# Cross attention weights turned on VectorE in 32x32 blocks, value product in sixteen 32x32 tiles of TensorE

## The reference

```
q, k, v = x@Wq.T + bq, x@Wk.T + bk, x@Wv.T + bv
attn    = sigmoid(layernorm(q) @ layernorm(k).T / 16 - log(1024))
x       = layernorm(x + (attn @ v @ Wo.T + bo) * layerscale)

qh, kh, vh = heads(x@wq.T + b), heads(ctx@wk.T + b), heads(ctx@wv.T + b)   # 16 heads of 16
attn    = softmax(qh @ kh.T / 4)                                            # 77 keys
x       = layernorm(x + (attn @ vh) @ dense.T + b)

r   = sigmoid((mu_r*x + (1-mu_r)*x_prev) @ W_r.T)
kk  = relu((mu_k*x + (1-mu_k)*x_prev) @ W_k.T) ** 2
out = layernorm(x + r * (kk @ W_v.T))
```

## Time and profile before

| | |
|---|---|
| median of 3 runs | 535.03 us (534.8 to 535.73) |
| span of the profiled execution | 531.8 us |
| PE busy | 515.0 us (97%), 4530 matmuls |
| ACT busy | 450.4 us (85%) |
| DVE busy | 443.7 us (83%) |
| POOL busy | 381.9 us (72%) |

### The profile page before, as it was taken

One profiled execution on the slowest core, in us unless ns is written; L12 is line 12 of the kernel. 1 busy time (PEld: TensorE's weight loads), 2 busy tenths in 40 slices (PEclk: granted clock), 3 DMA queues, 4 the chain that ended last, 5 costly groups with the idle time before them and its releaser, 6 DMA issues.

```text
span 531.8 us, 12709 instructions
## 1 busy us (share of the span) xinstructions
PE 515.0 (97%) x4530; PEld 468.3 (88%) x4530; DVE 443.7 (83%) x995; ACT 450.4 (85%) x1130; POOL 381.9 (72%) x554
## 2 busy tenths in 40 slices
PE   9999999999999999999999999999999898999994
PEld 6888999898989898989898989999898787899994
DVE  4787868878888879797979797778878888999996
ACT  3765579998989898989898989899999899898965
POOL 1774747676867676767667675767778889897996
PEclk9999999999999999999999999999999999999998
DMA  6410120110010110101010100020511000011122
GB/s 193 128 49 21 38 60 6 42 39 2 14 50 27 35 38 24 42 19 52 12 39 3 39 2 22 21 74 28 166 35 41 2 2 1 22 41 41 41 80 100
DMA packets 23269, 22.50 MB, mean 42 GB/s; under 512 B 1724, under 2 KB 23204, under 8 KB 23205
## 3 DMA queue, kind: packets, MB, share of 16 engines
q1 hardware_dynamic: 22770, 21.35, 12.7%
q10 hardware_dynamic: 434, 0.34, 0.2%
HBM read 14.55 MB, written 6.82 MB: 40 GB/s over the span
## 4 chain that ended last, share of the span: by engine, by line
PE 70%; ACT 12%; DVE 9%; issue 4%; POOL 4%; POOLq 0%; DVEq 0%; ACTq 0%
PE st L298 16%; PE acc L298 14%; PE xb L298 10%; PE proj L298 10%; PE xb L2077 5%; PE xb L2096 5%; ACT p_sb L594 4%; PE xb L2064 4%; DVE xm L1485 3%; ACT L545 2%; PE proj L1973 2%; PE xb L1885 1%; POOL rs L1110 1%; PE st L1893 1%; DVE kkT_lo L1299 1%
## 5 line engine op out<-in xcount | busy, mean ns | idle before, releaser
L594 ACT ACTIVATE p_sb<-xb,neg_mx 128x77 f32<-128x77 f32 x512 | 120.0, 366 | 5.2 <-DVE neg_mx L1412 4.9
L1047 POOL TENSOR_TENSOR fold<-p_sb 128x640 f32<-128x640 f32 x32 | 50.2, 1568 | 75.4 <-ACT p_sb L594 75.1
L1052 POOL TENSOR_TENSOR p_sb<-p_sb,rc 128x1280 f32<-128x1280 f32 x32 | 75.3, 2353 | 23.8 <-DVE rc L1425 23.7
L298 PE MATMUL acc<-vv_hi,aT_hi 128*128 128x256 f32 x256 | 76.6, 299 | 0.0
L545 ACT ACT_TABLE_LOAD x58 | 74.4, 1283 | 1.0
L298 PE MATMUL st<-qkT_hi 128*128 128x256 f32 x256 | 74.8, 292 | 0.0
L298 PE MATMUL st<-qkT_lo,qkT_hi 128*128 128x256 f32 x256 | 72.4, 283 | 0.0
L298 PE MATMUL st<-qkT_hi,qkT_lo 128*128 128x256 f32 x256 | 72.4, 283 | 0.0
L298 PE MATMUL acc<-vv_lo,aT_hi 128*128 128x256 f32 x256 | 72.2, 282 | 0.0
L298 PE MATMUL acc<-vv_hi,aT_lo 128*128 128x256 f32 x256 | 72.2, 282 | 0.0
L1412 DVE TENSOR_REDUCE neg_mx<-xb 128x4 f32<-128x308 f32 x128 | 53.7, 467 | 17.1 <-PE xb L2064 16.7
(11 more groups left out here) (262 smaller groups left out, 1707.9 us busy)
## 6 DMA issues: line engine op xcount, KB each, us to landing
xs<-in_x SPq DMA_DIRECT2D x16, 256.0 KB, 3.0
xraw<-in_xT SPq DMA_DIRECT2D x15, 256.0 KB, 2.9
out_y<-y SPq DMA_DIRECT2D x15, 256.0 KB, 2.1
x_kept<-xs SPq DMA_DIRECT2D x10, 256.0 KB, 2.2
x2s_a<-x_kept SPq DMA_DIRECT2D x2, 512.0 KB, 5.0
x2s_b<-x_kept SPq DMA_DIRECT2D x2, 512.0 KB, 7.1
x2s_c<-x_kept SPq DMA_DIRECT2D x1, 512.0 KB, 3.7
cT<-in_cT SPq DMA_DIRECT2D x1, 308.0 KB, 3.3
```

Of the source, the lines that this page charges most:

```text
L298: mm = pe.matmul(out, s_, m_, start=first and k == 0 and q == 0, stop=last and k == n - 1 and q == 2, skip_group_check=not check)
L594: ex = act.activation(weights(t)[:, h // KH * (H // 2) + KH * n + h % KH, 0:SC], logits[n][:, h * SC:(h + 1) * SC], ACT.Exp, bias=neg_mx[: ...
L1047: pool.tensor_tensor(fold[:].rearrange("p (h k) -> p h k", k=FO), p[:, :, 0:FO], p[:, :, FO:2 * FO], ALU.add).then_inc(fo_pool.sem, 1)
L1052: pool.tensor_tensor(weights(t), weights(t), rc[:, t % 2].rearrange("p (h o) -> p h o", o=1) .to_broadcast([P, H, SP]), ALU.mult).then_inc ...
```

## The change

1. `weights_t`, `weights_body` and both `weights_tail` go. In their place `weights_turn` (DVE, L1548) turns all 128 x 1280 weights of a tile in one instruction, each 32x32 block by itself, from `p_sb` into `pT`. The blocks stay in their group of 32 partitions, so a partition group of `pT` holds the keys for its own 32 tokens only.
2. `mixed` (PE, L2308) therefore works in 32x32 tiles: for each of 2 halves, 5 groups of 32 key slots, 4 groups of tokens and 4 groups of heads there is a matmul of 32 rows into 32 partitions with 64 columns: 160 for a pair where 16 were. The four groups of tokens go to the top 128 columns of the four `xb` banks, beside the logits (308 columns). `vb` grows from 2048 to 5120 elements per partition and holds the values four times, once for each partition group; 24 DMAs fill it.
3. `mixed_hi` and `mixed_lo` read the four banks through a pattern that puts the tokens back in order.
4. `cross_scores` no longer waits for turned weights; `exponentials(t)` waits for `weights_turn(t-2)`; `mixed` waits for all exponentials of the next tile, where it waited for three of four groups.
5. `table_for` issues the table load itself. The number of table loads in the program is 58 (59 before).
6. Every engine's list of calls is written in a new order. The rounds hold the same calls, apart from those above.

```diff
-                        w.wait_ge(*consts_pool.at(0))
-                        n = 8 * (next(spares) % NSPARE)
-                        act.activation(spare[:, n:n + 1], nlogs[:], func)
+                        act.preload_act_table(func)
...
-                        w.wait_ge(*tp_pe.at(t - NP))
+                        w.wait_ge(*tp_dve.at(t - NP))
...
-                def weights_body(t, c):
-                    w.wait_ge(*tp_pe.at(t, c + 1))
+                def weights_turn(t):
+                    w.wait_ge(*pn_pool.at(t))
                     w.wait_ge(*pads_pool.at(0))
...
-                    dve.tensor_copy(pT[:, 4 * c:4 * c + 4, (t % 2) * P:(t % 2 + 1) * P], tiles(tp_bank(c), 4))\
-                        .then_inc(tp_dve.sem, 1)
+                    dve.transpose(pT[:, t % 2], p_sb[:, t % NP]).then_inc(tp_dve.sem, 1)
...
-                    copy(oT[0][:], mixed_bank(i)).then_inc(pv_act.sem, 1)
+                    copy(by_token(oT[0][:]), by_quadrant(mixes_ps)).then_inc(pv_act.sem, 1)
...
                 def mixed(i):
                     b = i // JB
-                    for c in range(3):
-                        w.wait_ge(*turned(2 * i + 1, c))
+                    w.wait_ge(*tp_dve.at(2 * i + 1))
                     w.wait_ge(*vb_dma.at(VB_DMA - 1))
-                    if i < NJ - 2:
-                        w.wait_ge(*ex_act.at(2 * i + 2, 3))
...
+                    w.wait_ge(*ex_act.at(2 * i + 2 if i < NJ - 2 else NT - 1))
+                    if i:
+                        w.wait_ge(*pv_dve.at(i - 1))
+                        w.wait_ge(*xda_dve.at(min(i - 1, NJ - 3)))
                     for k in range(KC):
-                        for half in range(2):
-                            for n in range(4):
-                                mm = pe.matmul(mixed_bank(i)[32 * n:32 * (n + 1), k * D:(k + 1) * D], vb[:, n, half, :, :, KC * b + k].rearrange("p a d -> p (a d)"),
-                                               pT[:, 5 * k + n + half], start=half == 0, stop=half == 1, skip_group_check=True)
+                        for c in range(NC):
+                            for a in range(P // Q):
+                                own = slice(Q * a, Q * (a + 1))
+                                for n in range(NG):
+                                    slots = (NC * (NG * k + n) + c) * Q
+                                    mm = pe.matmul(xb[Q * n:Q * (n + 1), a, MX + 2 * Q * k:MX + 2 * Q * (k + 1)],
+                                                   vb[own, n, c, :, :, KC * b + k].rearrange("p a d -> p (a d)"),
+                                                   pT[own, :, slots:slots + Q], start=c == 0, stop=c == NC - 1, skip_group_check=True)
                     mm.then_inc(pv_pe.sem, 1)
...
                 def round_(r):
-                    at(attend, 4 * r - 18, NS, 9)
-                    at(scores, 4 * r - 15, NS, 13)
...
+                    qk(2 * r + 1)
+                    scores(4 * r - 11)
```

More of the change, by code:

```diff
@@ L89, in value_pieces @@
 def value_pieces():
-    for n in range(4):
[L92 to L98, removed]
+    for a in range(KH):
+        key = 0
+        while key < SC:
+            c, row = divmod(SP * a + key, Q)
+            count = min(Q - row, SC - key)
+            yield a, c, row, key, count
+            key += count
 def decoder_layer(nc, io):
@@ new lines, in _ @@
+                sigmoid_hi(16)
+                v_hi(7)
+                exponentials(4, 0)
+                exponentials(4, 1)
+                for r in range(6, 12):
+                    round_(r)
+                exponentials(16, 2)
+                tqk_hi(27)
+                exponentials(16, 3)
+                sigmoid(41)
+                xt_hi(15)
+                norm2(5)
+                sigmoid(42)
+                mixed_hi(7)
+                sigmoid_hi(41)
+                sigmoid_hi(42)
@@ L1735, in _ @@
-                weights_body(26, 0)
-                sigmoid_lo(61)
-                weights_body(26, 1)
+                qk_bias(16)
+                attended(3)
+                qk_stats(16)
+                sums(4)
+                mixed_lo(1)
+                stats1(3)
+                reciprocals(4)
+                maxima(5, 0)
+                maxima(5, 1)
+                maxima(5, 2)
+                for r in range(5, 11):
+                    round_(r)
+                v_bias(14)
+                qk_norm(28)
@@ new lines, in _ @@
+                qk_norm(31)
+                attended(11)
+                stats1(11)
+                sigmoid_lo(48)
+                sums(20)
+                mixed_lo(9)
+                reciprocals(20)
+                sigmoid_lo(49)
+                maxima(21, 0)
+                maxima(21, 1)
+                tqk_lo(31)
+                maxima(21, 2)
+                maxima(21, 3)
+                stats2(8)
+                sigmoid_lo(50)
+                x1_lo(11)
+                crossed(9)
@@ L2116, in x2 @@
                     if i == ND:
-                        for c in range(3):
-                            w.wait_ge(*turned(NT - 1, c))
+                        w.wait_ge(*pv_dve.at(NJ - 1))
                     elif i:
@@ new lines, in round_ @@
+                    cross_scores(2 * r - 10)
+                    scores(4 * r - 10)
+                    attend(4 * r - 14)
+                    tqk(2 * r + 1)
+                    attend(4 * r - 13)
+                    qk(2 * r + 2)
+                    mixed(r - 6)
+                    v(r + 1)
+                    cross_scores(2 * r - 9)
+                    scores(4 * r - 9)
+                    scores(4 * r - 8)
+                    attend(4 * r - 12)
+                    dense(r - 6)
+                    tqk(2 * r + 2)
@@ L2257, in _ @@
-                cross_scores(0)
                 attend(5)
-                scores(9)
+                attend(6)
+                attend(7)
+                cross_scores(1)
                 tqk(11)
-                attend(6)
                 scores(10)
                 qk(12)
-                cross_scores(1)
-                attend(7)
                 scores(11)
```

1347 lines of the change are left out of this document (750 added, 597 removed).

## The result

The changed kernel took **636.5 us** (median of 4 runs, 633.2 to 639.5) against 535.2 us (534.8 to 535.7): a ratio of **1.189**, interval 1.186 to 1.192. The forecast was 517.6 us in a range of 503 to 547. It is slower by 101 us, more than any rival had it (the worst was 600 us), and the profiled execution has a span of 634.6 us.

What follows compares the result with a forecast made beforehand. PE was taken to bound the kernel (busy 515.0 of 531.8 us). Sixteen pairs gaining 1.09 us each (4.26 less 3.17) save 17.4: span 514.4, plus 3.2 for a run, 517.6 us; range 503 to 547.

Steps and rivals of the forecast that it cites:

- 4.26 us a pair leave PE: On PE, 20 transposes (2.17 us) and the old value product (2.09 us) go from each pair.
- The body of the value product, 2.8 us: PE's 320 records a pair, taken between 2.1 and 3.5 us; with 0.37 for going in and out, 3.2 us.
- Code: PE's instruction fetch: 640 instructions are 2.5 packets at 1.2 us each; three one after the other take 3.5 us.
- the sign, stalls at every 256th instruction: In a value product on PE, starts 7 ns apart with such stalls would show code as the limit.
- Pace: PE issue between different tiles: 7 ns a record, from three gaps in `cross_scores`; 320 records take 2.1 to 2.2 us.
- The forecast's own point of no gain: On PE, a body of 3.9 us, 12 ns a record, from which the change is slower.
- Waits: PE's `mixed` waiting for exponentials fits with little to spare: nothing charged, up to 1 us a round kept in the range.
- rival 4: Gain eaten by `mixed`'s wait, DVE's longer blocks or code fetch: 528 to 533 us, chance 0.11; 535 to 550, chance 0.06.
- The turn: DVE's turn of 1280 elements takes 1.47 us, 47.0 us in all; DVE 22.3 us a middle round.
- SP's 24 DMAs: On SP, filling the larger `vb` takes 17.3 us instead of 8.9, about 74 to 91 us; cost nothing.
- Rival 3: A floor of some 25 ns per record on PE: body 8.0 us, +4.1 a pair, 600 us; chance 0.08.
- Rival 2: Only four tiles at a time on PE: body 4.5 us, +0.6 a pair, 545 us; chance 0.17.

Runs made afterwards that it cites:

- a_c2: Changed kernel with two of the five groups of key slots in the value product (256 instructions a pair, not 640), the rest left out: 528.7 us, ratio 0.988.
- a_c3: Changed kernel with three of the five groups of key slots in the value product (384 instructions a pair), the rest left out: 566.4 us, ratio 1.058.
- a_split: Changed kernel, whole computation, each value product in two halves of 320 instructions with up to two other calls between them: 630.1 us (622.0 and 638.2).
- a_far: Changed kernel, whole computation, second half of the value product some 8 us behind the first in the seven rounds of PE's loop: 609.2 us, ratio 1.139.
- b_cut8r: Kernel before, each value-product matmul cut into 8 along its columns, four tiles in turn, 512 instructions a pair: 599.3 us, ratio 1.120.
- b_cut8: Kernel before, each value-product matmul cut into 8 along its columns, eight in a row on the same tile, 512 instructions a pair: 705.2 us, ratio 1.318.
- b_cut4r: Kernel before, each value-product matmul cut into 4 along its columns, four tiles in turn, 256 instructions a pair: 541.2 us, ratio 1.011.
- a_cols128: Changed kernel with 128 columns instead of 64 in each of the 160 value-product matmuls, same 640 instructions: 634.1 us, ratio 1.186.

## Why the prediction was wrong

**4.26 us a pair leave PE: right.** In a_c2 PE is busy 119.38 / 5 = 23.9 us a round where the same sum had forecast 23.7. That PE then sets the period was right only with the holes counted: busy time and holes fill 32.2 of the changed kernel's 32.7 us, but in a_c2, without holes, PE idles 1.3 us a round.

**The body of the value product, 2.8 us: the step that failed.** From first to last start it is 7.9 us (302.39 to 310.28). Two terms were too small.
- *Code.* The prediction priced a packet at 1.2 us and let three in a row take 3.5. The 1.2 us was right for the transfer, 1.2 us for the packet of 307.5. But a transfer isn't the whole wait. It starts 1.1 to 1.7 us after PE enters the piece before, takes 0.9 to 1.3, and PE goes on 1.3 to 1.5 after its end: 3.73 us as the median of the fourteen middle pieces, 3.45 to 4.03. So the holes of this product are 4.0 us (3.6 a round on average) where 0.7 was charged. The Trainium skill, "Advanced Engine Details and Errata", section "ISA Cache", gives cache lines of 16 KB or 256 instructions, and only two of them. The trace agrees: pieces between two holes are of 256 instructions, and the most that ever ran ahead of a hole is 482 (241 records), under two lines. (Its 128 KB for TensorE would be eight lines; no run bears that out.) A first piece is then what is left of the line that PE is in and the whole next one, and how long it is depends on where in a line the product begins: 108 to 241 records in the changed kernel. So 256 instructions in a burst starve only where a line was entered just ahead of them (one product of a_c2, at 440 us), 384 starve for one line or, in three products of sixteen, for none, and 640 for two or one. The prediction named the sign, stalls at every 256th instruction, and had the size wrong.
- *Pace.* 7 ns came from three gaps between four matmuls after a wait. The first 32 records of the new product keep it, 128 in a row take 11.1 ns each. 320 would be 3.6 us, and the product with its way in and out 3.9: without any hole the pair would have gained 0.3 us, not 1.09. The forecast's own point of no gain was 12 ns a record.

**The clock: not in the prediction.** In the middle rounds of the changed kernel it is 0.90, in a_c2 1.00. It falls after the holes: the first line is a stretch behind the product of above, at 1.2 GHz throughout, the other two are the large products (L295) in five rounds of the changed kernel and of a_c2.

```profile
310.10:314.40 4.30, 4.30 (x55) 3.91 (x54) 1.56 (x5) 2.40 (x3) 1.31 (x5) 0.50 0.01 4
...
172.10:335.62 163.52, 107.87 (x721) 97.43 (x720) 0.90 0.09 26
...
182.59:308.30 125.71, 99.53 (x715) 89.96 (x714) 1.00 0.10 31
```

The same large products keep PE 21.6 us a round instead of 19.9, and with `cross_scores` the low clock costs 2.0 us a round. That closes the round: 23.9 us busy in a_c2, 2.7 more of value product, 2.0 of clock and 3.6 of holes (18.1 us in the five) are 32.2 of 32.7.

**Waits: too kind.** `mixed` does not wait as feared (2.5 us in all for the turn). But DVE needed 23.3 us a round in a_c2, not 22.3, by the collision with POOL, and waits for DVE's results (`oT_lo`, `qk_sb`) held the round at 25.1 us where PE's sum says 23.9. So a part of rival 4, the gain is eaten, came true as well: a_c2 is 528.7 us even with three fifths of the product left out. That this lies in its 528 to 533 is chance, since those were for the whole product.

**The sum, as it came:** 535.2 less 6.5 for all of the change with 256 instructions a pair (a_c2), plus 37.7 for the next 128 (a_c3), plus 70.2 for the last 256: 636.5. These are differences of runs and no mechanism. The holes alone are 53 us of the 101.

**Other terms.** The turn was right as sized, 1.50 us for 1.47, and 58 table loads stay. ACT has 22.9 us a round for 22.1, and is on no path. SP's 24 DMAs were put at nothing, and cost 2.2 us once: the last of them is issued at 100 us, not 91, its semaphore comes at 105.99, and the first product starts at 106.08. The profile calls this wait "issue" and names `vb` only in a_split, but in every kernel with the new `vb` the first product starts 0.1 us behind that semaphore.

**The rivals.** Rival 3 had the average right, 25 ns a record (8.1 us / 320), and the cause wrong: no floor per matmul, since 11.1 ns are held over 128 records. That its 600 us was the nearest number on record is luck. The range ended at 547 because the code was bounded at 3.5 us by the transfers alone. Rival 2's groups of four do not exist in the new tiles: the rows below are PE's starts up to 302.49 and up to 302.60 us, sixteen in the first 0.1 us, 7 ns apart, and sixteen more in the next.

```profile
302.39 0.37 PE L2308 MATMUL xb<-pT,vb 32*32 32x64 f32 x16
...
302.39 0.43 PE L2308 MATMUL xb<-pT,vb 32*32 32x64 f32 x32
```

**Still open.** What makes the granted clock fall. It goes with the two holes inside a product (after: 0.90) and not with the tiles (a_far: 1.00). b_cut8r, with one hole of 1.1 us on average, keeps 0.99, and is at 1.2 GHz behind its two longest, of 1.9 and 2.9 us (399.7 to 403.1 and 427.0 to 430.4 us, 0.50 each), but also once behind one of 0.8 us. The profile of a_split, with whole halves 4 us apart, has 0.92.

## What to carry to other kernels

Count instructions, not only columns: a burst of more than 256 on PE can starve for code, and it doesn't help that the average over a round is low. At 5.5 ns an instruction (the new tiles) and at 8 (b_cut8r) it did, at 25 (b_cut8) it did not; 3.73 us / 256 puts the border near 15, an estimate that no run tested. Before a matmul is cut into n pieces, ask how many packets of 256 the burst crosses, and what the pace is for the smaller pieces. b_cut4r and b_cut8r are one step apart, 6 us and 64 us, and only 18 of the 64 are holes.

A DMA queue's share gives how long the transfers take, not how long an engine waits for one: here 1.2 us against 3.73. And a reordered list has to be read for what it lays beside DVE's operations with two SBUF inputs on POOL, not only for its own engine.

## What the runs showed that was not expected

- A PE that is out of code resumes 3.73 us (3.45 to 4.03) after it last resumed, and the transfer of 16 KB is 1.2 us of that.
- Matmuls one after the other on the same 128x32 tile take 49 ns a record at 32 columns (b_cut8); with four such tiles in turn 16 (3.38 us less the 0.23 of the last one, over 196 gaps, in b_cut8r).
- On sixteen 32x32 tiles 11.1 ns a record at 64 columns, 13.8 at 128 (2.26 us from first to last start, over 164 gaps, a_cols128).
- A DVE operation with two SBUF inputs that overlaps one of POOL ends 0.55 us after it: 1.83 us for 0.69 beside an addition, 2.0 beside `fold`.
